# Logits of the attention mixing in a PSUM bank, one output bank in place of two, and the mixing steps spread over the VectorE's step table

## What is computed

```
q = _lin(xn, Wq, bq).reshape(b, n, H, HD) / np.sqrt(HD).astype(np.float32)
k = _lin(xn, Wk, bk).reshape(b, n, H, HD)
score = jax.nn.softmax(jnp.einsum('bihd,bjhd->bhij', q, k), axis=-1)
v = _lin(xn, Wv, bv).reshape(b, n, R, HD)
out = jnp.einsum('bhij,bjrd->bihrd', score, v)
...
comp = jnp.concatenate([qv, out], axis=-1) @ Ws.T + bs
comp = jax.nn.softmax(comp, axis=3)
out = (comp * out).sum(axis=3).reshape(b, n, DIM)
```

## Time and profile before

| | |
|---|---|
| median of 3 runs (lowest to highest) | 1370.21 us (1368.75 to 1371.03) |
| the profiled execution, own time | 1368.66 us |
| its span in the profile | 1366.8 us |
| PE busy | 1232.1 us, 90% of the span |
| DVE / ACT / POOL busy | 995.8 / 749.1 / 955.6 us |
| attention loop, first to last step | 66.4 us to about 1224.5 us of the span |

### The profile page before, as it was taken

The page is one execution under the profiler, slowest core; times in us unless marked ns, Lnnn a source line. Parts: engine busy times, 40 slices in busy tenths (PEclk is TensorE's granted clock), DMA queues, the critical chain, the costliest instruction groups (busy, mean ns, idle before and its releaser), DMA issues. The chain is left out here.

```text
span 1366.8 us, 27392 instructions
## 1 busy us (share of the span) xinstructions
PE 1232.1 (90%) x7869; PEld 565.0 (41%) x7869; DVE 995.8 (73%) x2115; ACT 749.1 (55%) x1463; POOL 955.6 (70%) x561
## 2 busy tenths in 40 slices
PE   4699989898989899898989898999999998986998
PEld 3144434343434344343434343444434343434675
DVE  6676777777777777677777777777777877775852
ACT  4066646565656556465656565665656565663443
POOL 4177868686878778686868687787868776873321
PEclk9599999999999999999999999999999999997999
DMA  5334434343444434343434344343434344330000
GB/s 125 103 66 108 101 83 108 78 107 66 106 94 101 99 74 100 74 106 77 107 67 107 90 103 97 74 107 86 103 73 103 82 96 92 79 62 16 16 23 24
DMA packets 60372, 115.52 MB, mean 85 GB/s; under 512 B 6656, under 2 KB 25568, under 8 KB 60336
## 3 DMA queue, kind: packets, MB, share of 16 engines
q0 software_dynamic: 18784, 67.70, 26.1%
q1 hardware_dynamic: 40770, 47.04, 10.8%
q10 hardware_dynamic: 782, 0.33, 0.1%
HBM read 22.51 MB, written 8.39 MB: 23 GB/s over the span
## 5 line engine op out<-in xcount | busy, mean ns | idle before, releaser
L1197 DVE TENSOR_REDUCE rowmax<-row_bank 128x1 f32<-128x512 f32 x1024 | 667.2, 684 | 273.0 <-PE row_bank L967 266.7
L1144 ACT ACTIVATE prob<-col_bank 128x512 f32<-128x512 f32 x1024 | 556.1, 597 | 425.4 <-PE col_bank L986 422.5
L996 PE MATMUL out_bank<-prob,v_op 128*64 128x512 f32 x2048 | 548.6, 607 | 0.2 <-ACT prob L1144 0.2
L1303 POOL TENSOR_TENSOR quad<-prob 128x1024 f32<-128x1024 f32 x128 | 335.3, 2619 | 110.0 <-ACT prob L1144 110.0
L967 PE MATMUL row_bank<-k_op,q_op 72*64 72x512 bf16 x2048 | 343.4, 397 | 74.1 <-DVE rowmax L1197 59.6
L1303 POOL TENSOR_TENSOR addend<-prob 128x1024 f32<-128x1024 f32 x128 | 320.7, 2505 | 94.5 <-ACT prob L1144 93.5
L986 PE MATMUL col_bank<-q_op,k_op 74*64 74x512 bf16 x2048 | 330.1, 390 | 15.0 <-ACT prob L1144 13.3
L986 PEld LDWEIGHTS col_bank<-q_op,k_op 74*64 74x64 bf16 x2048 | 123.3, 110 | 277.8 <-ACT prob L1144 155.4
L967 PEld LDWEIGHTS row_bank<-k_op,q_op 72*64 72x64 bf16 x2048 | 125.7, 110 | 228.4 <-DVE rowmax L1197 128.1
L996 PEld LDWEIGHTS out_bank<-prob,v_op 128*64 128x64 f32 x2048 | 163.2, 139 | 57.9 <-issue 3.3
L1308 POOL DMA_DIRECT2D quad<-addend x128 | 112.9, 882 | 77.5 <-POOL addend L1303 64.8
(11 more groups left out here) (187 smaller groups left out, 865.0 us busy)
## 6 DMA issues: line engine op xcount, KB each, us to landing
quad<-addend POOLq DMA_DIRECT2D x128, 512.0 KB, 5.3
v_op<-v_all SPq DMA_DIRECT2D x64, 256.0 KB
k_op<-k_parts SPq DMA_DIRECT2D x64, 144.0 KB
q_op<-q_parts SPq DMA_DIRECT2D x192, 48.0 KB
q_parts<-along_parts SPq DMA_DIRECT2D x11, 192.0 KB, 2.2
k_parts<-along_parts SPq DMA_DIRECT2D x33, 64.0 KB, 2.1
out<-y_out SPq DMA_DIRECT2D x8, 256.0 KB, 2.3
q_op<-max_rows SPq DMA_DIRECT2D x64, 4.0 KB
```

Of the source, the lines that this page charges most:

```text
L996: last = nc.tensor.matmul(out_bank[slot % 2][ih * VW:(ih + 1) * VW, :], v_op[slot][:, t, :], halves(prob[:, t, :])[:, :, ih, :], start=(t ...
L1144: nc.scalar.activation(prob[:, t, h * HALF:(h + 1) * HALF], col_bank[h][:, :], ACT.Exp).then_inc(exp_done, 1)
L1197: nc.vector.tensor_reduce(rowmax[:, parity, t, h:h + 1], row_bank[h][:, :], AX.X, ALU.max).then_inc(max_done, 1)
L1303: pool.tensor_tensor(dst, prob[:, 2 * k, :], prob[:, 2 * k + 1, :], ALU.add).then_inc(pair_done, 1)
```

## The change

1. The logits are worked in a PSUM bank, `logit_bank`: the sums are written there and every later step reads and writes it in place, as does ACT's Exp. Only the last step, "weights", writes the SBUF tile `logit`, because POOL reads it. The second operands (`rden`, `qs`, `top`, `total`) stay in SBUF.
2. To have that bank, the two out_banks become one and the two outTs one. `turn_out` now writes `turn_bank`, which the maxima, the projections and the denominators use too; waits keep them apart. `take_out` moves on ACT from step 1 to step 0, and PE waits for it (`outT_ready`) before the first `values` of the next unit in step 1.
3. Places move: `project.turn` from (1, 6) to (1, 4), `project.values` from (2, 6) to (3, 0), `mix.exps` from (2, 5) to (2, 3), `take_den` from (0, 7) to (0, 6), `take_values` from (3, 0) to (3, 1).
4. PLAN puts one mixing step into a step of the attention. The mixing of the last group runs behind the loop, in the SBUF tile as before.

```diff
+        self.work, self.total_work = self.logit[:, :, :], self.total[:, :]
...
         elif what == "logits over denominators":
             dve.wait_ge(self.logit_sum, TB * G + TB)
             dve.wait_ge(self.rden_ready, G + 1)
-            self.nc.vector.tensor_tensor(self.logit[:, :, :], self.logit[:, :, :], spread(flat(self.rden), R),
+            self.nc.vector.tensor_tensor(self.work, self.work, spread(flat(self.rden), R),
                                     ALU.mult).then_inc(self.logit_scaled, 1)
...
-        out_bank = [pb(f"out_bank{n}", [P, HALF]) for n in range(2)]
+        out_bank = pb("out_bank", [P, HALF])
+        logit_bank = pb("logit_bank", [P, HALF])
...
+        logits = TB * SLOTS * R
+        mix.work = logit_bank[:, 0:logits].rearrange("p (m r) -> p m r", r=R)
+        mix.total_work = logit_bank[:, logits:logits + TB * SLOTS]
...
-                    last = nc.tensor.transpose(out_bank[parity][:, c * P:(c + 1) * P],
-                                               outT[parity][:, c * P:(c + 1) * P], res.identf[:, :])
+                    last = nc.tensor.transpose(turn_bank[:, c * P:(c + 1) * P], outT[:, c * P:(c + 1) * P],
+                                               res.identf[:, :])
...
-                            if t == 1 and not (first and s < 2):
-                                pe.wait_ge(mix_in_ready, u - 1)
+                            if t == 1 and before:
+                                pe.wait_ge(outT_ready, u)
                             values(u, s, t - 1)
...
                             denominators(u - 1, sp_)
-                            turn_out(u - 1, sp_ % 2)
+                            if along and s == 1:
+                                pe.wait_ge(project.xnT_ready, G + 1)
+                            elif along and s == 2:
+                                pe.wait_ge(project.full_ready, 2 * G + 2)
+                            else:
+                                pe.wait_ge(max_rows_ready, u + (1 if last and s == SLOTS - 1 else 2))
+                            turn_out(u - 1)
...
-                        if t == 1 and before:
-                            take_out(u - 1, (s - 1) % 2)
+                        if t == 0 and before:
+                            take_out(u - 1, first and s == 1)
...
             PLAN = {
                 (1, 1): [("denominators",)],
-                (1, 4): [("logit sums", 0, 1)],
...
+                (1, 4): [("logit sums", 0, 2)],
+                (1, 5): [("logit sums", 2, 3)],
+                (1, 6): [("logit sums", 3, 7)],
+                (1, 7): [("logit sums", 7, 8), ("logits over denominators",)],
+                (2, 0): [("query part",)],
+                (2, 1): [("maxima",)],
+                (2, 2): [("shift",)],
+                (2, 4): [("totals",)],
+                (2, 5): [("normalizers",)],
+                (2, 6): [("weights",)],
                 (3, 4): [("output", 0, 1)],
...
+                (3, 5): [("output", 1, 2)],
+                (3, 6): [("output", 2, 6)],
+                (3, 7): [("output", 6, 8)],
             }
```

More of the change, by code:

```diff
@@ L407, in exps @@
         act.wait_ge(self.logit_shifted, G + 1)
-        self.nc.scalar.activation(self.logit[:, :, :], self.logit[:, :, :], ACT.Exp).then_inc(self.mix_exp, 1)
+        self.nc.scalar.activation(self.work, self.work, ACT.Exp).then_inc(self.mix_exp, 1)
 class FeedForwardWeights:
@@ L895, in attention @@
         onehot = sb("onehot", [P, SLOTS, 32])
-        outT = [sb(f"outT{n}", [P, HALF]) for n in range(2)]
+        outT = sb("outT", [P, HALF])
         denT = sb("denT", [P, HALF])
@@ L995, in values @@
                 for ih in range(2):
-                    last = nc.tensor.matmul(out_bank[slot % 2][ih * VW:(ih + 1) * VW, :], v_op[slot][:, t, :],
+                    last = nc.tensor.matmul(out_bank[ih * VW:(ih + 1) * VW, :], v_op[slot][:, t, :],
                                             halves(prob[:, t, :])[:, :, ih, :], start=(t == 0), stop=(t == TB - 1))
@@ L1050, in group @@
                                 pe.wait_ge(mix.den_ready, G)
-                            if s == 3 and along:
+                            elif s == 3 and along:
                                 pe.wait_ge(project.v_ready, G + 1)
+                            elif not (first and s < 2):
+                                pe.wait_ge(mix_in_ready, u - 1)
                             turn_max(u + 1, (s + 1) % 2)
@@ L1082, in group @@
                             project.qk(pe, G)
-                        if along and (s, t) == (2, 6):
+                        if along and (s, t) == (3, 0):
+                            pe.wait_ge(mix_in_ready, u - 1)
                             project.values(pe, G)
@@ L1154, in group @@
                             take_turned(u - 1, G if s > 0 else G - 1, (s - 1) % SLOTS)
-                        if t == 7 and s == 0 and not first:
+                        if t == 6 and s == 0 and not first:
                             take_den(G - 1)
-                        if t == 5 and s == 2 and not first:
+                        if t == 3 and s == 2 and not first:
                             mix.exps(act, G - 1)
@@ L1162, in group @@
                             project.normalize(act, G, (G + PAIRS_BEFORE) * PAIR, 1)
-                        if along and (s, t) == (1, 7):
+                        if along and (s, t) == (1, 5):
                             project.take_turned(act, G)
@@ L1217, in _ @@
                 (1, 1): [("denominators",)],
-                (1, 4): [("logit sums", 0, 1)],
-                (1, 5): [("logit sums", 1, 2)],
-                (1, 6): [("logit sums", 2, 5)],
-                (1, 7): [("logit sums", 5, 8)],
-                (2, 2): [("logits over denominators",), ("query part",)],
-                (2, 3): [("maxima",)],
-                (2, 4): [("shift",)],
-                (2, 6): [("totals",), ("normalizers",)],
-                (3, 0): [("weights",)],
+                (1, 4): [("logit sums", 0, 2)],
[8 more added lines that the diff above has]
+                (2, 6): [("weights",)],
                 (3, 4): [("output", 0, 1)],
-                (3, 5): [("output", 1, 3)],
-                (3, 6): [("output", 3, 5)],
-                (3, 7): [("output", 5, 8)],
+                (3, 5): [("output", 1, 2)],
+                (3, 6): [("output", 2, 6)],
+                (3, 7): [("output", 6, 8)],
             }
```

42 lines of the change are left out of this document (23 added, 19 removed).

## The result

The changed kernel takes **1270.48 us** (median of 4 runs, 1269.22 to 1270.81) against 1370.2 us before: a ratio of 0.9272, 95% interval 0.9256 to 0.9288. The prediction was 1274 us, 1258 to 1300.

The account below looks back on a forecast made before the run. PE was taken to bound the kernel, losing idle and slow-clock time in slot 2. Gains 92.0 + 6.6 - 2.0 = 96.6 us from 1368.66 give 1272, set at 1274 us for the median; range 1258 to 1300.

Parts of the forecast that it names:

- The stall and its cause: Slot 2: L347, with two SBUF operands, waits for POOL's additions; one PSUM source removes the wait; 92.0 us gained.
- today only L347: Mixing steps: of the five tensor_tensors, only this one meets POOL's L1303 in the kernel before; stated within the slower rival.
- The price of PSUM operands: Mixing steps on DVE: a PSUM source costs 0; bounds nothing or 0.1 us for each of 8 instructions.
- The output bank: Step 1: PE's values wait for ACT's copy of the unit before; 0.2 us where uncovered, 10 x 0.2 = 2.0 us lost.
- The 0.2 put into slot 2: Slot 2 of 14 groups: uncovered output bank turn, counted in the slot lengths 17.0 and 15.8 us.
- 766.43: Start of the next values, one step of 1.72 us later, leaving 0.70 us so that the output bank's turn just fits.
- The rival with 0.70 us a unit: Output bank: its turn costs the full 0.70 us in each of 63 units, 39 us more, giving 1313; chance 8%.
- The table: Step (3, 7): DVE sums two output tiles, not three, so slot 0 falls by 0.47 us in 14 groups, 6.6 us.
- Slot 3 of along groups: Stays 17.56 us, bound by ACT's 2.20 us wait for POOL's L211, which is what is late next.
- `project.turn` two steps earlier: Slot 1: the earlier turn needs the normalization of (1, 2), which is there; costed at 0.
- The slower rival: Mixing steps: the wait for POOL stays with one PSUM source, two more waits a group, 182 us, 1550; chance 4%.

Follow-up runs that it names:

- the kernel with one SBUF step: Changed kernel with logit sums written to the SBUF tile, so only the multiplication by rden has two SBUF operands; it still writes PSUM: 1322.36 us.
- the late copy: Changed kernel with ACT's copy of the output bank back behind the Exps of step 1: 1323.9 us, ratio 0.9664 against the kernel before.
- the run with the old split: Changed kernel with the output sums in slot 3 split into 1, 2, 2 and 3 tiles again: 1276.94 us.
- the old table in PSUM: Changed kernel, logits still in PSUM, with the earlier PLAN and the mixing Exp back in step (2, 5): 1287.18 us.
- the kernel with the single bank alone: Changed kernel with logits back in SBUF, the earlier PLAN and the mixing Exp in (2, 5); single output bank and moved projections stay: 1355.25 us.
- two edits of a few lines: Changed kernel with output sums split 1, 2, 4, 1 and ACT's second projection part moved from (3, 4) to (3, 5): 1257.96 us.

## Why the prediction was right, and where its terms were off

**The stall and its cause: right.** The forecast rested on the earlier trace rows for the cause and on one row, L631, for the cure. Slot 2 came out at 17.02 us where 17.0 was written, and 15.84 where 15.8 was. That the source in SBUF is what counts, and not the destination or the place, is shown by the kernel with one SBUF step. One reading was too narrow: "today only L347" waits is true of groups 1 to 10 and 14; in groups 11 to 13 of the kernel before L351 waited too.

The Trainium skill ("SBUF — State Buffer", § Who interferes with whom) says that a VectorE instruction with two SBUF inputs contends with a GpSimd instruction that reads SBUF. This case agrees: 2.70 against 0.43 us. Its lock that is held until the first instruction has finished is met too where POOL's additions don't overlap (1.49 us); where they do, the wait lasted for both.

**The price of PSUM operands: right at nothing.** The steps on 256 columns take 0.41 to 0.43 us in PSUM and in SBUF alike when they don't wait. The 65 ns by the table of op costs in the Trainium skill ("VectorE: DVE Perf Modes", the errata section) don't show in this kernel.

**The output bank: the term was too high.** The prediction took 0.2 us where nothing covers the copy. Slot 3 of group 12 shows 0.03 (15.62 for 15.59), so the 2.0 us of that term were well under 1. The 0.2 put into slot 2 are there (step (2, 1) takes 1.99 us for 1.73), but most of it as DVE's lateness: in group 0, where no logits are worked, that step takes 1.83. "766.43" for the next `values` wasn't read but added up from a step of 1.72 us; in the trace they start at 766.76, since that step was stretched already. The rival with 0.70 us a unit is out as long as the copy stands in step 0; the late copy shows what a turn that doesn't fit costs, 53 us.

**The table: right.** 0.47 us per group was predicted for slot 0, 0.46 measured in the changed kernel, and 6.5 us in the run with the old split. Slot 2 gains another 0.53 by it against the old table in PSUM.

**Slot 3 of along groups: right for the length, and right about what is late next.** 17.54 us, and moving ACT's wait by one step gave 12 us.

**What was costed at nothing and wasn't.** Slot 1 of along groups got 0.27 us longer, 10 times, 2.7 us. It is the step named "`project.turn` two steps earlier ... it is there": the input was there, and the price came from elsewhere. Only groups with `project.turn` show it; slot 1 of the others has the same length as before. By the starts of the `col` matmuls, step (1, 4) grew from 2.02 to 2.48 us and step (1, 6) shrank from 3.62 to 3.41. The kernel with the single bank alone has the same 17.21 us and the same steps with the old table and SBUF logits, so neither the table nor the logits' place is the cause. That the turn stood partly under other work in step 6 is my reading; no run tests it.

**What was missed.** At the loop's end PE waits for the last additions of POOL and their DMA: 9.45 us before, 6.11 now.

```profile
1235.86 1.93 PE L1007 MATMUL den_bank<-quad,onehot 128*32 128x512 f32 x8 [9.45 <-DMA quad<-addend]
```

```profile
1137.97 1.94 PE L1011 MATMUL den_bank<-quad,onehot 128*32 128x512 f32 x8 [6.11 <-DMA quad<-addend]
```

The prediction never followed the change beyond the loop. The gain there comes with the table, by POOL's product L401, as the kernel with the old table shows.

**The sum, and the luck in it.** By the profiled executions the slots 2 gave 91.7 us (92.0 predicted) and slot 0 6.7 (6.6). Of the 2.0 us for the bank nearly nothing was lost. The end of the loop gave 3.1 that wasn't predicted, slot 1 took 2.8 and the time before the loop 0.9. In all it is 97.8 us against 96.6, so two terms that were put at nothing, and missed, nearly cancel. The rest of the way from 1274 to 1270.5 is mostly the 1.55 us that I added because the profiled execution before was that much below its median; the one after was 0.3 above its own.

**The slower rival** asked for a wait with one PSUM source. Its condition never occurred: in each of groups 1 to 14 the five tensor_tensors ran beside a POOL addition, and none waited. But its price was wrong as well: with the logits in SBUF the three waits a group that it counted did come, and the kernel was no slower than before. It multiplied waits by the price of the longest one. In these runs a wait cost PE only what DVE's spare time didn't absorb, and what the clock added wasn't decided by its length alone.

## What to carry to other kernels

When one VectorE instruction lasts far longer than its twins, lay the GpSimd timeline over it before moving it: if both its tensor inputs are in SBUF and GpSimd works on SBUF, a PSUM home for one input takes the wait away, and spreading the instructions doesn't. Pay for the bank by looking for a pair of buffers whose turn fits into one step, and put the copy directly behind the last write, since one step later cost half of the gain. Then look at what the stall had covered; here two edits of a few lines were worth another 12.5 us, 11.9 of them by one of the two alone.

## What the runs showed of the hardware that I had not expected

- A DVE instruction that waits for POOL may have to wait for two POOL instructions: 4.07 us where the second began 0.17 us before the first ended, 1.49 us where it began 0.11 us after it. Both are so in each of groups 1 to 10 of their kernels. POOL's times in the profile are rough, so the order within these tenths of a microsecond isn't certain.
- The loss to the clock doesn't follow from the length of the idle time. In the kernel with the single bank alone, the same slot with the same waits had a granted clock of 1.00, 0.92 or 0.79 from group to group, 2.92, 2.94 and 2.73 us idle, and was 4.25 us apart between the best and the worst. Against 17.54 us in PSUM with the same table, a stall of some 3 us has a price from 2.7 to 7.0 us here.
